# A bank for each half of the transposed probabilities, one bank for values and output projection, and a projection that runs a tile later

## What is computed

```python
def attention(query, key, value, ...):           # 16 heads of 8 features
    q = split_heads(query @ Wq.T + bq)
    k = split_heads(key @ Wk.T + bk)
    v = split_heads(value @ Wv.T + bv)
    attn = softmax(einsum('bhsd,bhtd->bhst', q, k) / sqrt(8))
    out = einsum('bhst,bhtd->bhsd', attn, v)
    return out.transpose(0, 2, 1, 3).reshape(B, -1, D) @ Wo.T + bo

x = x + tanh(g_xattn[0]) * attention(layernorm(x), ctx, ctx, ...)        # layer 0
x = x + tanh(g_ffn[0])   * mixture_of_4_experts(layernorm(x), ...)
x = x + tanh(g_xattn[1]) * attention(layernorm(x), ctx, ctx, mask, ...)  # layer 1, masked
x = x + tanh(g_ffn[1])   * ternary_ffn_with_conv(layernorm(x), ...)
return x
```

## Time and profile before

| | |
|---|---|
| median of 3 runs | 987.94 us (987.78 to 988.53) |
| the profiled execution | 991.65 us, of which 989.9 us is the span from the first to the last instruction |
| PE busy | 947.1 us (96% of the span) |
| PE weight loads busy | 739.9 us (75%) |
| DVE busy | 833.3 us (84%) |
| ACT busy | 748.9 us (76%) |
| POOL busy | 588.4 us (59%) |
| attention of layer 0 (from the second tile's scores to the last tile's) | 18.1 to 268.0 us |
| attention of layer 1 (likewise) | 513.0 to 785.6 us |

### The profile page before, as it was taken

One profiled execution on the slowest core, in us unless ns is written; L12 is line 12 of the kernel. 1 busy time (PEld: TensorE's weight loads), 2 busy tenths in 40 slices (PEclk: granted clock), 3 DMA queues, 4 the chain that ended last, 5 costly groups with the idle time before them and its releaser, 6 DMA issues.

```text
span 989.9 us, 36747 instructions
## 1 busy us (share of the span) xinstructions
PE 947.1 (96%) x11854; PEld 739.9 (75%) x11854; DVE 833.3 (84%) x2349; ACT 748.9 (76%) x1709; POOL 588.4 (59%) x1232
## 2 busy tenths in 40 slices
PE   6999999999989999999899999999999899999997
PEld 4777777777779999998877677676777667777775
DVE  7888888889978888888887888888887778889886
ACT  5878787787787777766656777777777878888885
POOL 5545454544536555656885544545454378888884
PEclk9999999999999999999998999999999999999999
DMA  3501011100000000000000000000000000000001
GB/s 110 178 24 43 25 38 32 32 22 11 13 2 1 0 0 0 0 0 0 2 12 24 13 12 21 11 21 11 21 11 1 2 10 22 23 22 21 24 21 31
DMA packets 19361, 21.49 MB, mean 22 GB/s; under 512 B 3553, under 2 KB 12001, under 8 KB 19297
## 3 DMA queue, kind: packets, MB, share of 16 engines
q1 hardware_dynamic: 19296, 20.68, 6.9%
HBM read 16.48 MB, written 4.19 MB: 21 GB/s over the span
## 4 chain that ended last, share of the span: by engine, by line
PE 39%; issue 5%; POOL 4%; DVE 2%; ACT 2%; DVEq 0%; POOLq 0%; ACTq 0%
PE bank L1295 9%; PE bank L1318 7%; PE score L1372 4%; PE score L1579 2%; PE score L1581 2%; PE bank L1438 2%; PE score L1580 2%; PE score L1364 2%; PE bank L1342 2%; PE bank L1334 1%; PE bank L1330 1%; PE bank L1337 1%; ACT prob_t L599 1%; PE bank L1604 1%; POOL xdq L573 1%
## 5 line engine op out<-in xcount | busy, mean ns | idle before, releaser
L599 ACT ACTIVATE prob_t<-bank 128x512 f32<-128x512 f32 x256 | 152.8, 597 | 122.1 <-PE bank L1295 114.0
L952 DVE TENSOR_REDUCE smax<-score 128x16 f32<-128x1024 f32 x128 | 156.8, 1225 | 46.0 <-PE score L1372 30.2
L1295 PE MATMUL bank<-const,prob 128*128 128x128 f32 x1024 | 165.9, 285 | 14.1 <-ACT prob_t L599 14.1
L594 ACT ACTIVATE prob<-prob 128x512 f32<-128x512 f32 x256 | 161.2, 630 | 8.9 <-DVE prob L961 8.2
L1318 PEld LDWEIGHTS bank<-vb,prob_t 128*64 128x64 f32 x4096 | 130.4, 138 | 49.4 <-issue 42.9
L961 DVE TENSOR_TENSOR prob<-score,smax 128x512 f32<-128x512 f32 x256 | 165.0, 686 | 1.3
L1295 PEld LDWEIGHTS bank<-const,prob 128*128 128x128 f32 x1024 | 108.0, 141 | 67.6 <-issue 58.6
L1318 PE MATMUL bank<-vb,prob_t 128*64 128x18 f32 x4096 | 143.2, 213 | 0.0
L411 POOL TENSOR_SCALAR kj<-k_sb,const 128x512 f32<-128x512 f32 x124 | 85.5, 696 | 73.7 <-issue 38.5
L674 ACT ACTIVATE eb_t<-eb,gwt 128x128 f32<-128x128 f32 x256 | 81.4, 391 | 41.7 <-POOL eb_acc L452 24.7
L382 POOL TENSOR_TENSOR a_ve<-a_mv,const 128x4 f32<-128x4 f32 x32 | 6.5, 203 | 153.3 <-DVE a_mv L954 145.7
(11 more groups left out here) (162 smaller groups left out, 2334.6 us busy)
## 6 DMA issues: line engine op xcount, KB each, us to landing
ctx_t<-in_ctx SPq DMA_DIRECT2D x32, 256.0 KB, 2.7
x_all<-in_x SPq DMA_DIRECT2D x16, 256.0 KB, 2.8
out_x<-x_all SPq DMA_DIRECT2D x64, 64.0 KB, 1.5
ew<-in_ew SPq DMA_DIRECT2D x2, 512.0 KB, 5.8
f_cw<-in_f_cw SPq DMA_DIRECT2D x1, 768.0 KB, 7.9
w_t<-in_w_attn SPq DMA_DIRECT2D x2, 256.0 KB, 4.3
f_w<-in_f_w SPq DMA_DIRECT2D x2, 256.0 KB, 6.7
eb<-in_L_ffn_eb SPq DMA_DIRECT2D x1, 256.0 KB, 6.4
```

What stands on the lines that cost most here:

```text
L594: act.activation(v, v, ACT.Exp, scale=SCALE).then_inc(s["exp_done"], 1)
L599: act.activation(prob_t[:, 4 * half:4 * half + 4, :].rearrange("p i q -> p (i q)"), bank[PT], ACT.Copy).then_inc(s["p_copied"], 1)
L952: dve.tensor_reduce(smax[:].rearrange("p (r h) -> p r h", r=RH), sc, AX.X, ALU.max).then_inc(s["smax_done"], 1)
L1295: return pe.transpose(dst, src, ident)
```

## The change

Bank 7 is now called `PT2` and takes the second half of the transposed probabilities, so the halves do not share a bank. The transposed output and the projected output move to bank 6, beside the values' products (columns 256 to 383, `o_tr_ps`, and 384 to 511, `wo_ps`). With that every user of bank 6 must be kept apart by waits: `values` now waits for the residual sum of the tile three before it and for `copy_o`, `divide` for `copy_o`, `residual` for `copy_o`, `project_o` for the residual sum before. TensorE's step becomes scores, `values(n-2)`, `project_o(n-4)`, `transpose_o(n-3)`, both halves of `transpose_p(n-1)`, front. ScalarE's step becomes `copy_o(n-3)`, both `copy_p(n-1)`, both exponentials of tile n, front. VectorE's residual goes from the head of its step to the end of it, behind `divide`, with the same tile number, n-4. The tails are reordered in the same way, and the wait in layer 1 for the experts' last sums in banks 6 and 7 moves from step 2 to ahead of the first transposes in step 1. No arithmetic is added or taken away.

```diff
-PT, FRONT, OV, OW = 4, 5, 6, 7
+PT, FRONT, OV, PT2 = 4, 5, 6, 7
+        o_tr_ps, wo_ps = bank[OV][:, 2 * P:3 * P], bank[OV][:, 3 * P:4 * P]
...
             def copy_p(n, half):
-                               bank[PT], ACT.Copy).then_inc(s["p_copied"], 1)
+                               bank[(PT, PT2)[half]], ACT.Copy).then_inc(s["p_copied"], 1)
...
-                    if has(-1):
-                        exponentials(n - 1, o, 1)
-                        copy_p(n - 1, 0)
                     if has(-3):
                         copy_o(L, n - 3)
+                    if has(-1):
+                        copy_p(n - 1, 0)
+                        copy_p(n - 1, 1)
                     if has(0):
                         exponentials(n, par, 0)
-                    if has(-1):
-                        copy_p(n - 1, 1)
+                        exponentials(n, par, 1)
...
-            def residual(n, t):
+            def residual(n, t, read=None):
                 wait(dve, "wo_mm", n + 1)
+                wait(dve, "o_copied", n + 2 if read is None else read)
                 wait(dve, "bo_added", n + 1)
-                dve.tensor_tensor(x_tile(t), bank[OW][:, P:2 * P], x_tile(t), ALU.add).then_inc(s["x_attn"], 1)
+                dve.tensor_tensor(x_tile(t), wo_ps, x_tile(t), ALU.add).then_inc(s["x_attn"], 1)
             def divide(n, k):
                 wait(dve, "pv_mm", n + 1)
+                wait(dve, "o_copied", n)
                 wait(dve, "o_norm", n)
                 dve.reciprocal(rden[:], ov[:, :, HD]).then_inc(s["rden_done"], 1)
-                wait(dve, "o_tr", n - 1)
...
             def transpose_p(n, k, half):
-                wait(pe, "p_copied", 2 * n + half)
+                wait(pe, "p_copied", 2 * n + half - 1)
...
             def values(n, k):
                 wait(pe, "o_norm", n)
+                wait(pe, "x_attn", n - 2)
+                wait(pe, "o_copied", n - 1)
...
             def transpose_o(n, k):
                 wait(pe, "o_norm", n + 1)
-                wait(pe, "x_attn", n)
             def project_o(L, n):
                 wait(pe, "o_copied", n + 1)
+                wait(pe, "x_attn", n)
...
             def attention0_tail():
                 values(n, n % 8)
+                project_o(0, n - 2)
                 transpose_o(n - 1, n - 1)
                 pe.wait_ge(s["ew1_lo_done"], 2)
                 hidden(0, 0, 4, bank[0])
+                wait(pe, "o_norm", n + 1)
                 project_o(0, n - 1)
+                transpose_o(n, n)
                 hidden(0, 0, 5, bank[1])
-                transpose_o(n, n)
```

70 lines of the change are left out of this document (35 added, 35 removed).

## The result

The changed kernel took 977.04 us (median of five runs, 976.70 to 978.56), the kernel before 988.2 us on the same chip (987.78 to 989.78): 0.9867 of it, 95% interval 0.9839 to 0.9894. That is faster by 11.2 us, where 6.7 were forecast; the time lies in the stated range, 4.2 us under the forecast. The profiled execution took 977.75 us, 975.9 of it the span.

A forecast was written before the change was run, and what follows sets the result against it. TensorE's own order, near full load, was taken to set the pace, the one-bank round trip costing one step in four. Layers 8.2 us less, tails 1.5 back: 6.7 off 987.94 gave 981.2 us, range 976.0 to 989.3.

The forecast's parts named there:

- the round trip through one bank: TensorE's transpose, copy, transpose takes 1.49 us, making three steps 3.94 us each; a second bank removes it.
- the short step: Step with the front's transposes: 3.94 us falls to 3.57 in layer 0 and 3.90 in layer 1, bound by VectorE's subtraction.
- The values' wait for the residual sum: New wait of TensorE's values for VectorE's residual sum: in layer 0 once in four steps, in layer 1 none.
- the new neighbours on TensorE: Changed order of TensorE's pieces: taken at no difference; 0.05 us per tile either way would move the sum by 6.4 us.
- the release in layer 0: Values wait 0.17 us for the residual sum once in four steps, making the following step 4.09 us.
- the last steps of layer 1: Steps without a front: four give 0.7 us, limited by VectorE's 0.17 us idle each; the crowded step ahead gives 0.5.
- The tails' price: Projection of layer 0's last but one tile starts 1.0 us later, layer 1's tail loses 0.5: 1.5 us given back.
- Groups that cross a loop head: Five four-step groups per layer, where VectorE sets the pace: gain of 0.05 us each in layer 0, 0.15 in layer 1.
- Costed at nothing: ScalarE's moved copy_o and copies: no cost; if cover is gone, a wait once in four steps, under 2 us in all.
- Clock: Rival: layer 1's split idle stretch keeps the clock up at 520 us, 2.5 us more gained, 978.7 us; chance 0.17.
- No change: Rival: 0.05 us more per tile on TensorE, or VectorE's 3.74 us being 3.9, takes the gain; 987.6 us; chance 0.17.
- Slower by the release: Rival: release costing x above 0.14 us adds (x - 0.18) / 2 to some 60 steps; 990.8 us at 0.5; chance 0.13.

The follow-up runs named there:

- e5: Changed kernel, but in the one step of four with the values' front, that front stands between the transposes' halves again; 984.46 us, 0.9941 of before.
- e13: Changed kernel with one wait put back: VectorE's division product waits again for an earlier tile's transposed output; 976.1 us in a single execution.
- e9: e4 with VectorE's wait for GpSimd's normalisation factors moved from the statistics to the row maxima, one instruction later; 974.71 us.
- e16: e4 with VectorE's loops of both attention parts over 16 steps each time instead of 8; 972.28 us, 0.9827 of before.
- e8: The kernel before, unchanged, run again for a second profile; 987.54 us.
- e14: The changed kernel, unchanged, run again for a second profile; 976.67 us, 0.9865 of before.
- e4: Changed kernel with ScalarE's scaling of layer 1's output weights moved ahead of the eight bias products ending layer 0's tail; 974.77 us, 0.9848 of before.
- e2: e1 with both halves of the transposes in one bank again; 1035.9 us.
- e7: e4 with ScalarE's Silu table load in layer 1's tail moved behind the copies, quantisation and normalisation; 974.96 us.
- e12: e9 with the last but one tile's projection and the last transpose behind three more matmuls in each tail; 975.12 us.
- e6: Changed kernel with ScalarE's step in the order of before; 991.88 us, 1.0021 of before.
- e1: Changed kernel with the second half of the transposes back behind the front, keeping its own bank; 990.06 us, 0.999 of before.
- e3: Kernel before with five filler matmuls in layer 1 ahead of the third tile's mask, where TensorE idled 1.48 us; 989.48 us, 0.9982 of before.
- e10: Changed kernel with a spare VectorE reciprocal ahead of the division in each step, making the residual sum later; 979.66 us in a single execution.

## Where the prediction failed: the mechanism held, its sizes did not

The mechanism was right: the round trip through one bank was what made three steps alike, and with two banks the short step is bound by VectorE's subtraction, at 3.58 us (3.57 forecast) in layer 0 and 3.86 to 3.97 (3.90) in layer 1. The values' wait for the residual sum, where the trace of before had no row, came where it was placed, in the keys' step of layer 0.

The step of the prediction that failed is the size of the gain in the layers. It was put at 8.2 us and measured 14.1 (5.7 + 8.4). The largest miss is the term put at nothing, the new neighbours on TensorE: they gave 3.2 us. With it went the release in layer 0, priced at 0.17 us and measured at 0.04, and the last steps of layer 1, priced at 1.2 us and measured at 2.0. The tails' price, 1.5 us, was off as well. Two rows of the trace of before, which the prediction did not read, belong to point 1 (TensorE, the values' step of layer 0):

```profile
120.76 0.27 PE L1295 MATMUL bank<-const,o_n 128*128 128x128 f32 x1
120.97 1.15 PE L1342 MATMUL bank<-w_t,ctx_t 128*64 128x64 f32 x32
```

1. **The values' step**, kept at 4.25 and 4.58, took 4.14 and 4.47: 0.11 us in each of some 30 steps, 3.2 us. I had put the new neighbours at nothing, "since as many old pairs go", on one row of 0.02 us. The two rows above held the size: the values' front started 0.21 us after the transposed output, where another front needed 0.11 (125.01 to 125.12). e5 shows that the order is the cause, with 0.15 us per step for this one order. The prediction's bound of 0.05 us per tile would have covered it as a gain, but its centre did not.
2. **The release in layer 0**, put at 0.17 us once in four steps (4.09), cost 0.04 (3.97). The chain had VectorE's product 0.36 us behind the reciprocal, from before; the diff took a wait off that very instruction, and it came after 0.28. e13 puts the wait back and gets 0.35 and 4.06. I had listed the dropped wait in the change and priced it nowhere; without the drop, layer 0 would be 1.2 us longer and layer 1 0.8. The remaining 0.03 us go with the release itself, which took 0.11 us from the end of the residual sum to the values (124.18 to 124.29) and not 0.14.
3. **The last steps of layer 1** gave 2.0 us where 1.2 were forecast: 4.83 + 4.26 + 4.26 + 4.27 before, 3.81 + 3.93 + 3.93 + 3.93 after. VectorE's idle time of 0.17 us was not its whole reserve. Without its waits, and with the 0.07 of point 2, its own cycle is 3.93 us, 0.33 under the 4.26 of before; the step that ends a queue of work has to be rebuilt from starts, not from the idle figure. Groups that cross a loop head gave 0.12 and 0.30 us, where 0.05 and 0.15 were forecast, which is the 0.11 of point 1 again in the main; e9 and e16 show that what remains long there is the loop's turn.
4. **The tails.** In layer 0's, TensorE restarts 0.53 us later, counted from the last scores, where 1.0 was forecast (the new wait of 0.73 us is there, at 272.35). The rest of the +1.9 us in the table is the clock of single executions, as these pieces of the stretch show, in us (a group is the 16 matmuls `bank<-ew,hid_a`, of which the experts have 32):

| stretch between the layers | before | e8 | changed | e14 | e13 | e4 |
|---|---|---|---|---|---|---|
| last scores to restart | 16.06 | 16.07 | 16.59 | 16.60 | 16.73 | 14.35 |
| restart to 2nd group | 5.96 | 7.58 | 7.37 | 7.46 | 5.95 | 5.99 |
| 2nd to 28th group | 176.16 | 176.10 | 176.09 | 176.06 | 176.13 | 176.11 |
| 28th to 29th group | 22.37 | 20.78 | 22.41 | 22.42 | 20.78 | 22.44 |

The clock falls behind the restart or it does not, and again in front of the 29th group or not, and each fall costs 1.4 to 1.6 us. The second profile of before had one of the two, the first profile of before the other, the two of the changed kernel both, and e13, the changed kernel with one more wait, neither. So the tail's own price is 0.5 us, and whether the change makes either fall more likely is not shown. In layer 1's tail, put at 0.5 us, the next part's first matmuls start 0.35 us earlier after the last scores (3.73, 4.08 before), so the price is not there. The last part, to TensorE's last matmul, still took 1.5 to 2.4 us more in the two profiles, and 0.7 to 2.9 in the variants but e2, against the 201.4 of both profiles of before. In the changed kernel's first profile it is level with before 40 us in, and 1.3 us behind 67 us in. Neither e7 nor e12 moved it. Its cause is **open**.

"Costed at nothing", ScalarE's order, was right for the order made, but hid the most: undone alone it costs 14 us (e6), as much as the whole gain. So does TensorE's order (e1, 13 us). No run has the second bank with both old orders, so what it yields by itself is not shown; with either one undone nothing is left of the gain.

The rivals. **Clock**: the time came near its 978.7, but not for its reason. The prediction had named a changed clock row at 520 us as a sign that it was wrong, and the row did change: 1.00 in 515 to 525 us of the changed kernel. But the fall there was a matter of the one execution (e3, e8), so the sign says nothing either way. And since I had taken the 3.7 us between that execution and the median off as well, a clock that stays up was already in the median of before. That rival counted it twice. What "The HAM clock gate" of "TensorE: Matmul & The Clock Gate" in the Trainium skill says, that idleness takes the clock down, the rows at 277.75 us agree with. That it need not at this length, e13 shows: 2.52 us of idle time in the same place, and 1.00 behind it. **No change**: VectorE's 3.74 us did not rise, it fell to 3.67, except at a loop head, where the turn adds 0.49. **Slower by the release**: e10 gives its price, 0.11 us for 0.10 of delay, but in about 25 steps (the keys' and those at heads), not half of it in each of some 60. No run had the 0.4 or 0.5 us from which it would have decided.

## What to carry to other kernels

Here a bank for each half paid only together with the orders that let each engine use it, and undoing either order took the whole gain: test the parts of such a change singly, since their prices do not add up. For each wait that a diff drops, price the instruction that carried it, even if it never waited. And when a single profile lies above the median, find out what in it was slow before a gain there is put into a sum that starts from the median; compare two profiles piece by piece, and set the pieces where the clock fell in only one of them aside.

The version that beat both kernels is the changed one with ScalarE's weight scaling ahead of the bias products and VectorE's loops of 16 steps (e16): 972.28 us beside 976.67 for the changed kernel and 989.85 for the one before.

## What the runs showed of the hardware

- A wait for a second semaphore that has long been reached delayed VectorE's product, which also waits for the reciprocal just ahead of it, by 0.07 us (0.28 to 0.35, e13). A third wait on the reciprocal and on the residual sum did not show (1.20 and 0.22 us before and after).
- A turn of VectorE's loop delays its next instruction by 0.49 us (0.70 instead of 0.21; e9, e16).
- Four 128x128 transposes take 0.44 us ahead of four more (eight take 0.87 ahead of the front's), and 0.53 to 0.58 ahead of the values' front or the scores; the values' front takes 1.08 or 1.09 us whether scores or transposes follow (e5).
- Whether the granted clock falls is not settled by the idle stretch alone. Behind 2.52 us of idle time it showed 0.74 and 0.76 over 275 to 280 us in the two profiles of the changed kernel, and 1.00 in e13, e10 and e5; behind 2.6 us it stayed at 1.00 in the first profile of before and fell in the second (0.91 and 0.75 in 280 to 290 us). After 1.48 us it fell once and once not. The window of e13:

```profile
275.00:280.00 5.00, 2.48 (x14) 1.76 (x12) 2.87 (x15) 4.37 (x12) 1.23 (x3) 1.00 0.00 0
```

- One such fall among the experts costs 1.4 to 1.6 us (7.37 to 7.58 for a piece of 5.96, 22.4 for one of 20.78).
